# Graph network on one core: last rows three blocks later, first parts ahead of the widening, h rows stored four steps side by side, last layer's norm in pieces

## The reference

```python
def _graph_conv(x, W, b, src, dst, norm_src, norm_dst, n_nodes, act):
    h = x @ W
    m = h[src] * norm_src[:, None]
    agg = jax.ops.segment_sum(m, dst, num_segments=n_nodes)
    out = agg * norm_dst[:, None] + b
    return jax.nn.relu(out) if act else out
...
h = _graph_conv(feats, W1, b1, src, dst, norm_src, norm_dst, n, act=True)
h = _graph_conv(h, W2, b2, src, dst, norm_src, norm_dst, n, act=True)
h = _graph_conv(h, W3, b3, src, dst, norm_src, norm_dst, n, act=False)
...
x = _layernorm(x + h, axis=-1)
```

## Time and profile before

| What | Value |
|---|---|
| Time, median of 3 runs | 4119.0 us (4117.85 to 4121.85) |
| The profiled execution's own time | 4121.9 us |
| Its span | 4120.1 us |
| Counts stage: loop's first `hots` to the last matmul | 48.7 to 837 us |
| Layers stage: first matmul to last row stored | 855.7 to about 2055 us |
| Mean granted clock of TensorE | 0.874 of 2.4 GHz |
| Busy share of the span: PE, DVE, ACT, POOL | 80%, 80%, 69%, 47% |

### The profile page before, as it was taken

One profiled execution on the slowest core, in us unless ns is written; L12 is line 12 of the kernel. 1 busy time (PEld: TensorE's weight loads), 2 busy tenths in 40 slices (PEclk: granted clock), 3 DMA queues, 4 the chain that ended last, 5 costly groups with the idle time before them and its releaser, 6 DMA issues. The chain is left out here.

```text
span 4120.1 us, 61173 instructions
## 1 busy us (share of the span) xinstructions
PE 3280.7 (80%) x21477; PEld 2653.8 (64%) x21477; DVE 3279.5 (80%) x5077; ACT 2858.0 (69%) x3071; POOL 1924.1 (47%) x1883
## 2 busy tenths in 40 slices
PE   4888888869999999999677777777777777777763
PEld 3777777748887888788556555555555555555553
DVE  9999999945555555555569989898899889889895
ACT  3666666534444444444399999999999999999974
POOL 7122200050210121021277777777777777777764
PEclk7888888879999999999888888888888888888875
DMA  4344433368987898899578777777777777777752
GB/s 137 129 136 132 134 126 123 132 229 296 306 308 271 300 310 302 278 319 321 179 213 219 217 212 210 211 212 209 206 218 209 210 209 213 209 207 215 205 166 75
DMA packets 363341, 876.56 MB, mean 213 GB/s; under 512 B 54730, under 2 KB 213695, under 8 KB 363175
## 3 DMA queue, kind: packets, MB, share of 16 engines
q1 hardware_dynamic: 272471, 739.80, 55.8%
q0 software_dynamic: 59936, 119.71, 12.4%
q10 hardware_dynamic: 30768, 15.26, 1.2%
HBM read 653.46 MB, written 221.09 MB: 212 GB/s over the span
## 5 line engine op out<-in xcount | busy, mean ns | idle before, releaser
L1144 POOL DMA_INDIRECT hgat<-x_rows,edge_src x1564 | 1476.1, 944 | 490.0 <-issue 489.4
L864 PE MATMUL psum<-wide,hp 128*128 128x490 f32 x4704 | 1104.2, 396 | 57.0 <-DVE hp L952 33.0
L864 PEld LDWEIGHTS psum<-wide,hp 128*128 128x128 f32 x4704 | 890.0, 190 | 252.2 <-DVE hp L952 36.0
L800 ACT CAST wide<-gran 128x1470 fp32r<-128x1470 bf16 x336 | 478.0, 1423 | 611.6 <-PE psum L864 607.5
L947 DVE CAST wide<-gran 128x1960 fp32r<-128x1960 bf16 x336 | 446.5, 1330 | 445.5 <-PE psum L864 439.9
L609 PEld LDWEIGHTS psum<-hi_hot,lo_hot 128*128 128x128 bf16 x7840 | 545.3, 155 | 217.8 <-issue 68.3
L1325 DVE TENSOR_SCALAR psum<-rows_e,edge_same,edge_first 128x128 f32<-128x128 f32 x1564 | 644.9, 412 | 42.5
L525 ACT CAST stage<-psum 128x490 bf16<-128x490 f32 x784 | 451.3, 576 | 308.2 <-PE psum L609 297.6
L609 PE MATMUL psum<-hi_hot,lo_hot 128*128 128x49 bf16 x7840 | 573.5, 219 | 94.8 <-DVE hi_hot L401 93.3
L773 POOL DMA_INDIRECT x_sb<-h_rows,last_i x147 | 175.1, 1191 | 951.2 <-DMA h_rows<-h_out 916.7
L1249 PE MATMUL psum<-c_b,one_b 96*128 96x512 bf16 x391 | 186.7, 477 | 508.0 <-DVE prod_e L1307 498.9
(11 more groups left out here) (220 smaller groups left out, 3661.1 us busy)
## 6 DMA issues: line engine op xcount, KB each, us to landing
gran<-step_counts SPq DMA_DIRECT2D x336, 857.5 KB, 5.7
dist<-weight_by_step SPq DMA_DIRECT2D x195, 512.0 KB, 6.4
running_products<-rows_e SPq DMA_DIRECT2D x195, 512.0 KB, 3.2
step_counts<-stage SPq DMA_DIRECT2D x112, 857.5 KB, 5.0
ef<-in_edge_attr SPq DMA_DIRECT2D x195, 448.0 KB
hgat<-x_rows,edge_src POOLq DMA_INDIRECT x1564
kn<-keep_and_norm_of_steps SPq DMA_DIRECT2D x48, 490.0 KB, 7.3
ef<-in_edge_attr SPq DMA_DIRECT2D x171, 64.0 KB
```

Of the source, the lines that this page charges most:

```text
L800: nc.scalar.copy(wide[:, i % WIDE, :, NEARC:SB], gran[:, i % RING, :, NEARC:SB]).then_inc(s_wf, 1)
L864: last = nc.tensor.matmul(y, hps[:, 7 * g + i, part, :], wide[:, r, :, i * IS:(i + 1) * IS], start=first, stop=last_)
L1144: pool.indirect_dma_start(out=hgat[:, f % U, c, :], out_offset=None, in_=x1_d, in_offset=bass.IndirectOffsetOnAxis(ap=edge_src[:, 2 * f + ...
```

## The change

Five pieces, all in the order of the work or in how rows lie:

1. `last_rows` runs in block 4, granule 3, in place of block 1, granule 3.
2. In the first layer, `scale_h(0, 0)`, `scale_h(0, 1)`, `rest_h(0, 0)` on DVE and `part(0, 0)` on ACT stand ahead of the first two widenings.
3. `times_w` takes every fourth step (t, t + 4, ...) into each of its four matmuls, so that a partition of `h_out` holds four neighbouring steps. `store_h` then writes 122 partitions of 2048 bytes and one of 1024 bytes; PE, DVE and ACT work on 123 partitions there.
4. Last layer: `reciprocals(0)` and `root(0)` go to block 46, the 35 `normalise` operations are split in five pieces of 7 (block 46, g == 5 and 6; block 47, g == 2 to 4), `layer_norm(5)` and that of tiles 42 to 44 go into block 47 (g == 5, 6), and behind the last block only the tiles 45 to 48 are left to be summed; stores are split accordingly.
5. In the counts stage the four operations for `edge_same` and `edge_first` go ahead of `read_rows(0)`.

```diff
-                    read_rows(0)
                     dve.wait_ge(s_sin, 1)
                     link(nc.vector.tensor_scalar(e_ang, e_ang, 0.5, 0.5, ALU.mult, ALU.add))
...
                     link(nc.vector.tensor_tensor(first_k, e_ang, same_k, ALU.subtract))
+                    read_rows(0)
...
-            scaled = sbt("scaled", [P, SB])
+            RQ = -(-SB // 4)
+            scaled = sbt("scaled", [P, 4 * RQ])
...
+            LATE = next(t for t in range(NT) if blocks_for(t) == BLOCKS)
...
-            CUTS = (0, 35, NT)
+            NORMS = [(7 * q, 7 * q + 7) for q in range(6)] + [(42, LATE), (LATE, NT)]
+            CUTS = (0, 35, LATE, NT)
+            NORMS_TO = (5, 7, 8)
+            STORES = [(7 * q, 7 * q + 7) for q in range(5)] + [(35, LATE), (LATE, NT)]
...
-                        act.dma_start(of_block[:, 0:3 * P, :].rearrange("o (t p) d -> p (o t) d", p=P), h_out[:, r, 0:3, :]
+                        whole = SB // 4
+                        act.dma_start(of_block[:, 0:4 * whole, :].rearrange("o (p t) d -> p (o t) d", t=4),
+                                      h_out[0:whole, r]).then_inc(s_hst[r], 16)
+                        act.dma_start(of_block[:, 4 * whole:SB, :], h_out[whole:RQ, r, 0:SB - 4 * whole, :]
                                       ).then_inc(s_hst[r], 16)
-                        act.dma_start(of_block[:, 3 * P:SB, :].rearrange("o p d -> (o p) d"),
-                                      h_out[4 * P - SB:P, r, 3, :]).then_inc(s_hst[r], 16)
...
+                    part(0, 0)
                     widen(0)
                     widen(1)
...
-                            if n == 3 * BLOCKS - 1 and g == 2:
+                            if n == 3 * BLOCKS - 2 and g == 4:
                                 root(0)
-                            if n == 3 * BLOCKS - 1 and g == 6:
-                                for q in range(5):
-                                    store_x1(q)
+                            if n == 3 * BLOCKS - 1:
+                                if g == 1:
+                                    store_x1(0)
+                                    store_x1(1)
+                                elif g == 6:
+                                    for i in range(2, 5):
+                                        store_x1(i)
+                                    root(1)
...
-                        for t, a in enumerate((0, P, 2 * P, SB - P)):
-                            last = nc.tensor.matmul(rows[:, t * D:(t + 1) * D], scaled[:, a:a + P], ws[k][:],
+                        every_fourth = scaled[:].rearrange("p (q t) -> p t q", t=4)
+                        for t in range(4):
+                            last = nc.tensor.matmul(rows[0:RQ, t * D:(t + 1) * D], every_fourth[:, t, :], ws[k][:],
                                                     start=True, stop=True)
...
+                    scale_h(0, 0)
+                    scale_h(0, 1)
+                    rest_h(0, 0)
                     widen(0)
                     widen(1)
...
-                            if n == 1 and g == 3:
+                            if n == 4 and g == 3:
                                 last_rows()
...
-                            if n == 3 * BLOCKS - 1 and g == 1:
-                                reciprocals(0)
-                            if n == 3 * BLOCKS - 1 and g == 3:
-                                normalise(0)
+                            if n == 3 * BLOCKS - 2:
+                                if g == 3:
+                                    reciprocals(0)
+                                elif g >= 5:
+                                    normalise(g - 5)
+                            if n == 3 * BLOCKS - 1:
+                                if 2 <= g <= 4:
+                                    normalise(g)
+                                elif g == 5:
+                                    layer_norm(5)
+                                elif g == 6:
+                                    layer_norm(6)
+                                    reciprocals(1)
                     post(At(3 * BLOCKS - 1))
                     bias_rows(2, At(3 * BLOCKS - 1))
-                    layer_norm(5)
-                    layer_norm(6)
-                    reciprocals(1)
-                    normalise(1)
+                    normalise(5)
+                    layer_norm(7)
+                    reciprocals(2)
+                    normalise(6)
```

More of the change, by code:

```diff
@@ L661, in gnn @@
             s_xg = [sem(f"s_x_gathered{q}") for q in range(NG7)]
+            s_xl = sem("s_x_last_gathered")
             s_hm, s_p1, s_hp = (sem(n) for n in ("s_h_scaled", "s_part1", "s_part2"))
@@ L701, in value, with gathered @@
                     return c if self.reg is None else self.reg * (self.step * mul) + c
-            CUTS = (0, 35, NT)
+            NORMS = [(7 * q, 7 * q + 7) for q in range(6)] + [(42, LATE), (LATE, NT)]
+            CUTS = (0, 35, LATE, NT)
+            NORMS_TO = (5, 7, 8)
+            STORES = [(7 * q, 7 * q + 7) for q in range(5)] + [(35, LATE), (LATE, NT)]
+            def gathered(engine, q, k, last_too):
+                early = 7 if q < 6 else LATE - 42
+                engine.wait_ge(s_xg[q], 16 * early * k)
+                if q == 6 and last_too:
+                    engine.wait_ge(s_xl, 16 * (NT - LATE) * k)
             with nc.Block() as block:
@@ L774, in _ @@
                                                     in_offset=bass.IndirectOffsetOnAxis(ap=last_i[:, t:t + 1], axis=0)
-                                                    ).then_inc(s_xg[t // NG7], 16)
+                                                    ).then_inc(s_xg[t // NG7] if t < LATE else s_xl, 16)
                 @block.scalar
@@ L829, in _ @@
                             if n == 0:
-                                part(0, g)
+                                if g:
+                                    part(0, g)
                             elif b == 0 and g in (2, 6):
@@ L836, in _ @@
                                 widen(NG7 * n + g + 1)
-                            if n == 3 * BLOCKS - 1 and g == 2:
+                            if n == 3 * BLOCKS - 2 and g == 4:
                                 root(0)
-                            if n == 3 * BLOCKS - 1 and g == 6:
-                                for q in range(5):
-                                    store_x1(q)
+                            if n == 3 * BLOCKS - 1:
[6 more added lines that the diff above has]
+                                    root(1)
                     copy_h(2, At(BLOCKS * 3 - 1))
                     store_h(At(BLOCKS * 3 - 1), At(BLOCKS - 1))
-                    root(1)
-                    for q in range(5, NG7):
-                        store_x1(q)
-                    act.wait_ge(s_x1d, 16 * NG7)
+                    store_x1(5)
+                    root(2)
+                    store_x1(6)
+                    act.wait_ge(s_x1d, 16 * len(STORES))
                     for r in range(2):
@@ L920, in post @@
                         dve.wait_ge(s_z, m.value(1, 1))
-                        nc.vector.tensor_tensor(scaled[:], seg[:, r, :], kn[:, r, 1, :], ALU.mult).then_inc(s_scaled, 1)
+                        nc.vector.tensor_tensor(scaled[:, 0:SB], seg[:, r, :], kn[:, r, 1, :], ALU.mult).then_inc(s_scaled, 1)
                     def bias_rows(k, m):
                         dve.wait_ge(s_z, m.value(1, 2))
-                        rows = rbanks[m.parity()][:].rearrange("p (t d) -> p t d", d=D)
-                        nc.vector.tensor_tensor(rows, rows, b_all[k][:].unsqueeze(1).to_broadcast([P, 4, D]), ALU.add
+                        rows = rbanks[m.parity()][0:RQ].rearrange("p (t d) -> p t d", d=D)
+                        nc.vector.tensor_tensor(rows, rows, b_all[k][0:RQ].unsqueeze(1).to_broadcast([RQ, 4, D]), ALU.add
                                                 ).then_inc(s_zrow, 1)
@@ L969, in first_bias, with layer_norm @@
                         link(nc.vector.tensor_scalar(c1_turned[:], c1_sb[:], -1.0, SOFT_MAX, ALU.mult, ALU.add))
[L971 to L972 removed]
+                    def layer_norm(i):
+                        a, b = NORMS[i]
+                        q = a // 7
                         dve.wait_ge(s_xr[q % 2], 16 * (q // 2 + 1 + q // 6))
[L974 to L979 removed]
+                        gathered(dve, q, 3, b == NT)
+                        nc.vector.tensor_tensor(x_sb[:, a:b, :], x_sb[:, a:b, :], x_again[:, q % 2, a - 7 * q:b - 7 * q],
+                                                ALU.add).then_inc(s_ln, 1)
+                        dve.wait_ge(s_ln, i + 1)
+                        if i:
+                            dve.wait_ge(s_bn, 2 * i)
                         for t in range(a, b):
@@ L994, in normalise @@
                     def normalise(i):
-                        dve.wait_ge(s_sd, i + 1)
-                        for t in range(CUTS[i], CUTS[i + 1]):
+                        a, b = STORES[i]
```

(12 more changed lines are left out.)

27 lines of the change are left out of this document (10 added, 17 removed).

## The result

| | before | after |
|---|---|---|
| Median (7 runs each, one chip) | 4120.5 us (4117.9 to 4122.8) | 4133.7 us (4131.7 to 4136.1) |
| Ratio | | 1.003, 95% interval 1.0021 to 1.0039 |
| Profiled execution, its span | 4121.9, 4120.1 us | 4133.1, 4131.1 us |

The change makes the kernel 13 us (0.3%) slower, where 22.5 us less were forecast; 4133.7 lies outside the range of 4072 to 4118. Some later runs took over 4490 us, the kernel before too, because the edges stage, which no kernel here changes, ran at a lower granted clock (0.73 or 0.79 where it is 0.85 here, over 2100 to 4000 us): totals are therefore set against before on the same chip, and otherwise the layers stage is compared by its scans.

A forecast was written before the change was run, and what follows sets the result against it. PE was taken as the bound, transfers close behind. The terms -21.7 - 5.8 - 0.3 - 6.5 - 4.2 + 3.0 + 12 + 1 sum to -22.5, from the median 4119.0 to 4096; own range 4086 to 4108, wider 4072 to 4118.

The forecast's parts named there:

- Strided weights, +1: `times_w` loading every fourth f32 column, 8 loads a block: between 0 and 22.7 us, taken as 1 us more.
- a beat above 23.5 us with L898's loads grown: Sign in the steady blocks, where 23.41 us a block was the beat, that would prove the forecast wrong.
- The rival that the stride costs what rows 10 allow: Weight loads on PE pay 18 to 22 us, by profiled strided and unstrided load times: 4115 us, no change; 8%.
- Stores of h rows, +15: 122-partition stores run on two engines: 3.0 us more at the end, 12 more for both layer changes.
- Last rows, -21.7: Block 1 no longer waits at `last_rows` for the gathers of `pairs` and falls to the beat: 21.7 us less.
- First parts ahead, -5.8: Start of the layers stage: PE starts 5.7 us earlier and granule 7 just fits; 5.8 us less, bounds 3.5 and 6.3.
- Its rival had feared granule loads: The early start is lost to granule loads and a late sum of tiles 42 to 44: 5 us less won, 4101; 8%.
- Order of the counts stage, -0.3: Four operations fill DVE's idle time ahead of `read_rows(0)`; the loop's first `hots` starts at 48.4: 0.3 us less.
- Last block, -6.5: Block 47, 6.51 us above the beat, with `normalise` split into pieces of 7: 6.5 us less, up to 3 fewer won.
- The end, -4.2 + 3.0 = -1.2: Behind the last block: smaller sums, normalising and last store, 4.2 us less; the two-engine store of h rows, 3.0 more.
- The rival in which the stores take all engines: All 16 engines take the h-row store, so the end and both layer changes gain: -44, 4075 us; 12%.
- The rival in which two engines fall behind with the granules: In every block the two storing engines delay granule loads, then widening and PE: slower, 4141 us; 12%.

The follow-up runs named there:

- rows alone: The kernel before with only the third piece (strided weight loads, stores of 2048-byte partitions) put in; its four times, 4577 to 5185 us, give no verdict.
- old rows: The changed kernel with its third piece undone: weight loads, rows and stores of h as before; second run 0.9943 of before, first unclear.
- spread: The changed kernel with the 122-partition store cut into 112 and 10, weight loads still strided; 4120.5 us, 0.9996 of before.
- packed kernel: The changed kernel, but DVE writes `scaled` so that each weight load reads neighbouring columns, stores as changed; 4508.5 us, 0.9946 of before on its chip.
- both mends: The changed kernel with neighbouring weight columns and the 122-partition store cut into 112 and 10; 4081.2 us, 0.9901 of before.
- small loads later: On both mends: filter constants' loads moved from ahead of granule 7 behind block 3, `first_bias` to block 6, old counts order; 4080.6 us, 0.9901 of before.

## Why the prediction was wrong

**Strided weights, +1: this step failed.** The stride of 16 bytes in the weight loads was put at +1 us; it measured 0.787 x 43 = 33.8 us in the steady blocks and about 36 with blocks 16, 32 and 47. Even the upper bound, 22.7, was too low. The sign that the prediction named for it, a beat above 23.5 us with L898's loads grown, is what came. The step held two mistakes:

- *The wrong row gave the size.* I took 157 - 98 = 59 ns from bf16 loads. The loads in question are f32; they took 192 ns before (the row of L875), twice 98, and 321 after, about twice 157. With the difference doubled too, the bound would have been 8 x 0.118 x 48 = 45 us.
- *The overlap was misread.* From one load of L609 in 99 ns I concluded that the stride lengthens a load more than the spacing. But that row doesn't show what the spacing would be without the stride. Here spacing grew from 1.09/8 = 136 to 1.88/8 = 235 ns, by 99, and the load by 129. Three quarters of the stride's price reach PE, which has no idle time in these blocks.

The rival that the stride costs what rows 10 allow named the mechanism, with 8% and 4115 us. The Trainium skill (SBUF — State Buffer, "Door 1") says that accesses need two hits in a line of 16 bytes for full rate. The loads agree: at 8 bytes, two hits, nothing; at 12 bytes a part; from 16 bytes on, one hit, all of it (that 24 bytes take 304 ns, less than 16, it doesn't tell). By its other phrase, that four fp32 can be strided for free, the 321 ns would not be there, and the measurement decides against that reading.

**Stores of h rows, +15: right in kind, too large.** Two engines it was: 0.13 of 16 while the store ran, and cutting it so that 112 partitions go on 16 engines took 5.1 us off. The end's store took 8.20 us where 7.4 was forecast. The store to `x_rows` that shared the two engines is not the reason: in rows alone, where it is not under way, it took 8.13. The forecast let each engine move 25 GB/s throughout; there it was 16 to 25. At the layer changes the gathers came 10.3 and 10.4 us after the issue, not 12. PE stood 4.5 us longer in block 32 (9.51 for 5.06) and 1.1 in block 16 (9.73 for 8.67), not 6 each. The first of them was already 12.1 us in the trace before (store issue 1261.08, gather 1273.14), a row that I had not read; I had carried the shorter one over. The Trainium skill's rule (DMA: Bandwidth & Descriptors, "Why a DMA increments its semaphore by 16 and not by 1") gives two engines for 122 partitions and 16 for 112, and the traces agree with both.

**Last rows, -21.7: right**, 21.70, but to the hundredth only by luck: block 1 holds 0.8 us of the stride, and 0.9 is won back there from a scan 0 that was late (22.49 us with old rows, 23.40 with the small loads moved). In block 4 it costs nothing: that block takes a beat.

**First parts ahead, -5.8: 3.5**, the lower bound. The early start came, but granule 7 was late. Its rival had feared granule loads; what held SP's queue were the small loads ahead of granule 7. With these moved, scan 0 comes 1.8 us sooner, of which block 1 gives back 0.6. That is a small part of the miss of 36 us.

**Order of the counts stage, -0.3: nothing.** The first `hots` stood at 48.65 to 49.72 in the old order and at 48.85 to 49.71 in the new one, over all runs. The prediction let the rows arrive as before; they came 2.6 us later. Three of the gathers of rows (from 29.5 us on) took 2.92, 2.21 and 1.52 us on POOL where they had taken 2.48, 0.94 and 0.94, and they now run beside the four operations of DVE. In the kernel before the gathers beside the same four operations are slow too (1.94, 2.21, 1.52, 1.52 us). That the operations slow them is likely by this, but no run tests it.

**Last block, -6.5: 4.9** in the kernel after. The missing 1.6 are 0.8 of the stride and 0.8 of a sum that waited for the slow store (spread, the block takes a beat, 24.20). With old rows the block takes 23.40, so the full 6.5.

**The end, -4.2 + 3.0 = -1.2: +0.3.** From the first gather to the edges stage it is 4.3 us shorter (17.6 to 13.3), as forecast; the store takes 3.8 more (4.43 to 8.20) and not 3.0; and from the last scan to the store's issue there are 0.85 more (4.55 to 5.40), whose cause stays open. The -1.1 of the ledger lies in stages that nothing here changes.

**The sum as it should have been:** with the measured stride in the place of +1, -22.5 + 35 = +12.5, against +13.2 measured; the too large price of the stores and what the start, the last block and the end won less about cancel, by luck. The packed kernel shows the same from the other side: by an estimate from its last scan 4133.7 - 35.8 = 4097.9, where 4096 was forecast; its measured ratio, 0.9946, gives 4098. The rival in which the stores take all engines needs the kernel with both mends: 4081.2, where 4075 was given. The rival in which two engines fall behind with the granules is refuted by DMA at 0.86 and a beat that packed columns bring back to 23.40 with the same stores.

## What to carry to other kernels

Where PE has no idle time, a weight load of f32 at a stride of 12 bytes or more is paid in every block: let an engine with room lay the columns out, and price a load by a row of the same type and form, not by the nearest name. A store's time depends first on how many engines take it: cut 122 partitions into 112 and 10 before making its runs longer. A change of layout has two ends; the profile of the bound engine's instructions is to be read for both.

## What the runs showed that I had not expected

- The price of a strided f32 weight load rises between 8 and 16 bytes and stays there: 192 ns at 8 bytes, 249 at 12, 321 at 16, 304 at 24, 325 at 32.
- On DVE the multiply of 492 columns grew by 0.38 us (0.67 to 1.05) when both its inputs were read at a stride of 16 bytes; PE pays 0.79 us for reading as many columns at that stride.
- A block's store has 126 packets where it had 508 (on q10 12432 in all for 30768), and the closing one still took almost twice as long, as two engines carried it.
- One small load of a column (L754, 128 partitions of 4 bytes) held SP's queue for 5.82 us behind the first seven granules. It is the place and not the load: issued behind block 3 it took 0.50 us (the row below, small loads later), and in its absence the three bias loads behind the granules took 6.06 (3.73 in packed and spread). What holds the queue there is not shown.

```profile
940.98 0.50 SPq L763 DMA_DIRECT2D c_sb<-in_L_gnn_b  x1
```
